# An audio tower of patch tokens, attention and routed experts on one core: places in five products, one joint inverse deviation, and another order of the first two rounds

## The reference, cut to what matters

```python
# tokenizer: x is (128, 1000, 16); 124 patches of 16 steps x 16 features at stride 8
y = einsum('bpi,di->bpd', patches, W) + b           # 256 -> 256
h = (y - mean(y)) * rsqrt(var(y) + 1e-5) * gamma + beta
# attention over the 124 tokens of each of 128 sequences, one head of 256
a = layernorm(h)
q, k, v = a @ Wq.T + bq, a @ Wk.T + bk, a @ Wv.T + bv
h = h + softmax(q @ k.T / scale) @ v
# experts: 6, the two best of each token, three layers 256x256
f = layernorm(h)
p = softmax(relu(f @ rw1 + rb1) @ rw2 + rb2); top_w, top_i = top_k(p, 2)
g = softmax(top_w)
e = relu(relu(f @ w1 + b1) @ w2 + b2) @ w3 + b3     # per expert
h = h + sum(g * e[top_i])
```

## Time and profile before

| | |
|---|---|
| median of three runs | 1258.8 us (1256.7 to 1262.85) |
| the profiled execution's own time | 1265.46 us |
| its span | 1263.7 us |
| instructions | 28188 |
| granted TensorE clock, mean | 0.981 |
| busy: PE, PEld, DVE, ACT, POOL | 96%, 85%, 79%, 71%, 73% |
| stage A (round 5 to 31) | about 101 to 557 us |
| end of stage A mixed with the first tiles | to about 665 us |
| stage B alone | 665 us to the end |

### The profile page before, as it was taken

One profiled execution on the slowest core, in us unless ns is written; L12 is line 12 of the kernel. 1 busy time (PEld: TensorE's weight loads), 2 busy tenths in 40 slices (PEclk: granted clock), 3 DMA queues, 4 the chain that ended last, 5 costly groups with the idle time before them and its releaser, 6 DMA issues.

```text
span 1263.7 us, 28188 instructions
## 1 busy us (share of the span) xinstructions
PE 1207.0 (96%) x7888; PEld 1073.8 (85%) x7888; DVE 998.4 (79%) x3283; ACT 894.7 (71%) x2094; POOL 918.5 (73%) x740
## 2 busy tenths in 40 slices
PE   4899999999999999999779999999999999999994
PEld 4799888988889888988668888888988888888883
DVE  4578888888889888887677878787777878777783
ACT  3688888888888888886446676666667666666762
POOL 2127888888888888888788676777677767766776
PEclk9899999999999999999898999999999999999997
DMA  3234555645445545654489979767786696787655
GB/s 101 85 123 123 151 154 158 153 124 127 124 127 130 131 122 134 180 160 120 130 184 267 243 137 219 133 108 128 148 199 116 114 234 116 128 192 156 115 60 58
DMA packets 137191, 180.44 MB, mean 143 GB/s; under 512 B 38344, under 2 KB 103500, under 8 KB 137036
## 3 DMA queue, kind: packets, MB, share of 16 engines
q0 software_dynamic: 75456, 69.19, 34.3%
q1 hardware_dynamic: 60316, 108.67, 28.5%
q10 hardware_dynamic: 1264, 0.79, 0.2%
HBM read 159.01 MB, written 101.49 MB: 206 GB/s over the span
## 4 chain that ended last, share of the span: by engine, by line
PE 86%; DVE 5%; ACT 4%; issue 3%; POOL 1%; DMA 0%; POOLq 0%; SPq 0%; ACTq 0%; DVEq 0%
PE bank L784 29%; PE bank L580 18%; PE bank L811 15%; PE bank L773 4%; PE bank L729 4%; PE bank L715 4%; PE bank L631 4%; PE bank L622 2%; PE bank L672 2%; PE bank L737 2%; PE bank L707 1%; PE bank L659 1%; ACT rec L885 1%; ACT square L920 1%; DVE h L1188 1%
## 5 line engine op out<-in xcount | busy, mean ns | idle before, releaser
L566 POOL DMA_INDIRECT out<-yo,tail x268 | 431.3, 1609 | 173.3 <-issue 139.9
L517 POOL DMA_INDIRECT expert_rows<-rec,row_i x256 | 358.5, 1401 | 72.8 <-issue 61.0
L995 ACT ACTIVATE h2v<-bank,small 128x512 f32<-128x512 f32 x134 | 92.3, 690 | 205.2 <-PE bank L784 190.6
L811 PE MATMUL bank<-w_sb,h_hi 128*128 128x256 f32 x1072 | 210.2, 289 | 3.0 <-issue 3.0
L784 PE MATMUL bank<-h_hi,w_sb 128*128 128x512 f32 x536 | 178.8, 394 | 7.6 <-issue 7.6
L784 PE MATMUL bank<-x_hi,w_sb 128*128 128x512 f32 x536 | 178.3, 394 | 4.6 <-DVE x_lo L1366 4.6
L811 PEld LDWEIGHTS bank<-w_sb,h_hi 128*128 128x128 f32 x1072 | 172.6, 193 | 3.7 <-issue 3.6
L811 PE MATMUL bank<-w_sb,h_lo 128*128 128x256 f32 x536 | 152.2, 284 | 0.0
L784 PEld LDWEIGHTS bank<-h_hi,w_sb 128*128 128x128 f32 x536 | 102.0, 190 | 28.1 <-issue 8.0
L784 PEld LDWEIGHTS bank<-x_hi,w_sb 128*128 128x128 f32 x536 | 101.8, 190 | 26.2 <-issue 4.9
L1381 DVE CAST h_hi<-h1v 128x512 fp32r<-128x512 f32 x134 | 63.2, 472 | 71.1 <-ACT h1v L988 71.1
(11 more groups left out here) (198 smaller groups left out, 3034.1 us busy)
## 6 DMA issues: line engine op xcount, KB each, us to landing
w_sb<-split_weights SPq DMA_DIRECT2D x189, 512.0 KB
xg<-expert_rows SPq DMA_DIRECT2D x67, 530.0 KB
out<-h SPq DMA_DIRECT2D x32, 496.0 KB
split_weights<-half_w SPq DMA_DIRECT2D x36, 256.0 KB
small<-in_esmall SPq DMA_DIRECT2D x67, 134.0 KB
x_in<-in_x SPq DMA_DIRECT2D x32, 250.0 KB
expert_rows<-pad_rows SPq DMA_DIRECT2D x9, 530.0 KB
raw_w<-in_eweights SPq DMA_DIRECT2D x36, 128.0 KB
```

Source lines behind the costliest of these rows:

```text
L517: pool.indirect_dma_start(rows_dram, bass.IndirectOffsetOnAxis(ap=row_i[0:TOK, slot, j, k:k + 1], axis=0), rec[0:TOK, slot, j, :], None).t ...
L566: pool.indirect_dma_start(out, bass.IndirectOffsetOnAxis(ap=tail[:, t % TAILS, j, E8:].bitcast(I32), axis=0), yo[:, t % YO, j, :], None, c ...
L811: mm = pe.matmul(banks[6 + b][:, (j % 2) * D:(j % 2 + 1) * D], act[:, c, j * P:(j + 1) * P], w[:, 2, c, wh, :], start=(c == 0 and p == 0), ...
L995: act.activation(h2v[:, m, :], banks[bank + m][:], ACT.Relu, bias=small[:, t % SLOTS, DC + m:DC + m + 1]).then_inc(S["h2_v"], 1)
```

## The change

- The places are made by five products. `picked` gets a fifth block of eight columns, always zero; the triangular product and four products with ones run over 40 columns, so that the fifth block of the result is the total of the group.
- GpSimd makes the inverse deviations of norm 0 (group of xa) and norm 2 (group of x2) in one pair of operations over both, behind norm 1's inverse and all three leftover scatters. ScalarE's squares are scaled by D ** -0.5 and put their sum into `mv`, where the other norms keep their variance. The three semaphores become `rstd13` and `rstd2`.
- VectorE compares the expert numbers as they come from `max_index`, without the copy `choice`, and makes the token numbers in one operation.
- At the start the token weight is centred by one sum and one fused operation, without waiting for the bias. The bias is loaded into a cleared tile (SP waits for GpSimd's first memset) and is handled behind the weight and behind the first input halves on both engines.
- `fold` is cut in two on TensorE and VectorE. On TensorE the first part stands ahead of round 0's token products and the second behind them. On VectorE the first part and `nmr` (now `shifts`) stand behind the statistics of x0, ahead of the input and chunk halves; the second stays at the end of the round.

```diff
+        def deviations(it):
+            return 2 * (it + 2)
...
             sp.dma_start(proj_raw["tok"][:], ...).then_inc(S["tok_loaded"], 16)
+            sp.wait_ge(S["pool_const"], 1)
             for r in (0, 32):
-                sp.dma_start(bias_raw["tok"][r:r + 1, :], tok_b).then_inc(S["tok_loaded"], 16)
+                sp.dma_start(bias_raw["tok"][r:r + 1, :], tok_b).then_inc(S["tok_bias_loaded"], 16)
...
+            pool.memset(bias_raw["tok"][0:33, :], 0.0).then_inc(done, 1)
...
+            def inverse_std(norms, ready, n):
+                count = len(range(NORMS)[norms])
+                pool.tensor_scalar(vareps[0:TOK, norms, :], mv[0:TOK, norms, :, 1], EPS, None, ALU.add).then_inc(ready, 1)
+                pool.wait_ge(ready, n * 2 + 1)
+                pool.tensor_tensor(rstd[0:TOK, norms, :], vareps[0:TOK, norms, :],
+                                   neghalf[0:TOK, :].unsqueeze(1).to_broadcast([TOK, count, GB]), ALU.pow
+                                   ).then_inc(ready, 1)
...
-                    inverse_std(1, S["rstd2"], g)
+                    inverse_std(slice(1, 2), S["rstd2"], g)
                 if x5:
-                    scatter(x5[0], range(5, 7))
+                    scatter(x5[0], range(5, 8))
                 if xa:
                     wait_apart(pool, S["squares"], (g + 1) * GB, S["pool_passed"])
-                    inverse_std(0, S["rstd1"], g)
-                if x5:
-                    scatter(x5[0], range(7, 8))
                 if x2:
                     wait(pool, S["xn2_ready"], g * GB)
                     wait_apart(pool, S["av"], g * AV_N + 1 + 3 * GB, S["pool_passed"])
-                    inverse_std(2, S["rstd3"], g)
+                if xa or x2:
+                    inverse_std(slice(0, NORMS, 2) if xa and x2 else slice(0, 1) if xa else slice(2, NORMS),
+                                S["rstd13"], it + 1)
...
+                if it == 0:
+                    fold_weights()          # TensorE, ahead of the token products
                 if xa:
                     if it == -1:
-                        pe.wait_ge(S["proj_low"], 2)
+                        pe.wait_ge(S["proj_low"], 1)
...
+                            if it == -1:
+                                pe.wait_ge(S["proj_low"], 2)
                             mm = pe.matmul(into, ones_r[:, 0:TOK], bias_row["tok"][:], start=False, stop=True)
                 if it == 0:
-                    fold()
+                    fold_rest()
...
-                    W = GB * E8
+                    W = (GB + 1) * E8
                     pe.matmul(banks[3][0:TOK, 0:W], before[0:TOK, 0:TOK], picked[0:TOK, :], start=True, stop=False, ...)
-                    for k in range(1, GB):
-                        pe.matmul(banks[3][0:TOK, k * E8:W], ones[0:TOK, 0:TOK], picked[0:TOK, 0:W - k * E8], ...)
-                    for k in range(GB):
-                        mm = pe.matmul(banks[3][0:TOK, W:W + E8], ones[0:TOK, 0:TOK], picked[0:TOK, k * E8:(k + 1) * E8], ...)
+                    for k in range(1, GB + 1):
+                        mm = pe.matmul(banks[3][0:TOK, k * E8:W], ones[0:TOK, 0:TOK], picked[0:TOK, 0:W - k * E8], ...)
...
+                if it == -2:                # ScalarE, behind xT_hi of group 0
+                    act.wait_ge(S["centred"], 2)
+                    high_halves("tok")
+                    act.wait_ge(S["centred"], 4)
+                    act.wait_ge(S["pool_const"], 3)
+                    high_bias("tok")
...
                         act.activation(square[0:TOK, :], ..., ACT.Square,
-                                       accum_out=sumsq[0:TOK, j:j + 1]).then_inc(S["squares"], 1)
+                                       scale=D ** -0.5, accum_out=mv[0:TOK, 0, j, 1:2]).then_inc(S["squares"], 1)
...
                 v.tensor_reduce(tok_mean[:], proj_raw["tok"][:], AX_X, ALU.add).then_inc(s, 1)
-                v.tensor_scalar(tok_mean[:], tok_mean[:], 1.0 / D, None, ALU.mult).then_inc(s, 1)
-                for c in range(DC):
-                    v.tensor_scalar(proj_raw["tok"][:, c, :], proj_raw["tok"][:, c, :], tok_mean[:, c:c + 1], None,
-                                    ALU.subtract).then_inc(s, 1)
+                v.scalar_tensor_tensor(out=proj_raw["tok"][:], in0=tok_mean[:].unsqueeze(2).to_broadcast([P, DC, D]),
+                                       scalar=-1.0 / D, in1=proj_raw["tok"][:], op0=ALU.mult, op1=ALU.add).then_inc(s, 1)
...
                     statistics(1, ...)      # VectorE, x0
+                if it == 0:
+                    fold_weights()
+                    shifts(0)
...
+                if it == -2:                # VectorE, behind xT_lo of group 0
+                    low_halves("tok", 1)
+                    centre_bias()
+                    low_bias("tok", 2)
+                    v.wait_ge(S["pool_const"], 22)
...
-                v.tensor_copy(choice[R, :, :], mxi[R, :, 0:TOPK]).then_inc(s, 1)
-                                choice[R, :, :].unsqueeze(3).to_broadcast([TOK, GB, TOPK, E8]),
+                                mxi[R, :, 0:TOPK].unsqueeze(3).to_broadcast([TOK, GB, TOPK, E8]),
...
-                v.tensor_copy(rec[R, g % SENT, :, D + E8:REC].bitcast(I32), tokid[R, :].unsqueeze(2)).then_inc(s, 1)
-                v.tensor_scalar(tokid[R, :], tokid[R, :], float(GT), None, ALU.add).then_inc(s, 1)
+                v.tensor_scalar(rec[R, g % SENT, :, D + E8:REC].bitcast(I32), tokid[R, :].unsqueeze(2), float(g * GT), None,
+                                ALU.add).then_inc(s, 1)
```

More of the change, by code:

```diff
@@ L60 @@
 SMALL = 2 * DC + D + E8
-LN1_N, AV_N, TOPK_N, POS_N = 15, 14, 25, 4
+LN1_N, AV_N, TOPK_N, POS_N = 15, 14, 23, 4
 ADDED = 16 * TB
@@ L69 @@
 PADS_AT, TABLE_AT = 1, 20
+NORMS = 3
 DRAIN = G + 1
@@ L472, in _ @@
             pool.memset(ones[:], 1.0).then_inc(done, 1)
-            pool.wait_ge(done, 6)
+            pool.wait_ge(done, 7)
             pool.affine_select(out=ident[:], in_=ident[:], compare_op=ALU.not_equal, fill=1.0, base=0,
@@ L493, in _ @@
             pool.memset(xg[:, 0, :, :], 0.0).then_inc(done, 1)
-            pool.wait_ge(done, 18)
+            pool.wait_ge(done, 19)
             pool.iota(xg[:, 0, :, D + E8:REC].bitcast(I32).rearrange("p j o -> p (j o)"), [[1, TB]], base=NTOK + TILE,
@@ L498, in _ @@
                       channel_multiplier=TB).then_inc(done, 1)
-            def inverse_std(which, ready, g):
-                if which == 0:
-                    pool.tensor_scalar(vareps[0:TOK, which, :], sumsq[0:TOK, :], 1.0 / D, EPS, ALU.mult,
-                                       ALU.add).then_inc(ready, 1)
-                else:
-                    pool.tensor_scalar(vareps[0:TOK, which, :], mv[0:TOK, which, :, 1], EPS, None,
-                                       ALU.add).then_inc(ready, 1)
-                pool.wait_ge(ready, g * 2 + 1)
-                pool.tensor_tensor(rstd[0:TOK, which, :], vareps[0:TOK, which, :], neghalf[0:TOK, :],
-                                   ALU.pow).then_inc(ready, 1)
+            pool.memset(picked[:], 0.0).then_inc(done, 1)
+            def inverse_std(norms, ready, n):
[5 more added lines that the diff above has]
+                                   ).then_inc(ready, 1)
             def scatter(g, pieces):
@@ L581, in product, with fold_weights @@
                 return mm
-            def fold():
-                one = ones_r[:].bitcast(F32)
+            one = ones_r[:].bitcast(F32)
+            def fold_weights():
                 pe.wait_ge(S["const_loaded"], N_CONST)
@@ L1063, in statistics, with fold_weights @@
                     v.bn_aggr(mv[R, which, j, :], stats[R, which, j, :]).then_inc(s, 1)
-            def fold():
+            def fold_weights():
                 s = S["fold_sb"]
+                v.reciprocal(invs_col[:], scale_col[:]).then_inc(S["invs"], 1)
                 v.wait_ge(S["fold_ps"], 1)
@@ L1174, in step @@
                                     half_w[:, n % RING, 0, :].bitcast(F32), ALU.subtract).then_inc(S["w_low"], 1)
-                if x0:
-                    g, slot, rnd = x0
-                    v.wait_ge(S["rstd2"], g * 2 + 2)
-                    v.scalar_tensor_tensor(out=nmr[R, 0, :], in0=mv[R, 1, :, 0], scalar=-1.0, in1=rstd[R, 1, :],
-                                           op0=ALU.mult, op1=ALU.mult).then_inc(S["ln1"], 1)
+                if x0 and it > 0:
+                    shifts(x0[0])
                 if it == DRAIN - 2:
@@ L1206, in step @@
                 if it == 0:
-                    v.wait_ge(S["const_loaded"], N_CONST)
-                    v.reciprocal(invs_col[:], scale_col[:]).then_inc(S["invs"], 1)
-                    fold()
-                    low_halves("v", 4)
-                    v.wait_ge(S["proj_high"], 5)
+                    fold_rest()
+                    low_halves("v", 3)
+                    v.wait_ge(S["proj_high"], 4)
                     v.tensor_tensor(proj["q"][:, 1, :, :], qk_raw[:], proj["q"][:, 0, :, :].bitcast(F32),
```

(4 more changed lines are left out.)

77 lines of the change are left out of this document (31 added, 46 removed).

## The result

The changed kernel takes **1249.6 us** (median of five runs, 1248.2 to 1249.8), the kernel before beside it on the same chip 1260.6 us (five runs, 1256.7 to 1262.9). The ratio is 0.9913, with a 95% interval of 0.9895 to 0.9931: 11.0 us less, where 11.7 were forecast. The profiled execution took 1249.82 us around a span of 1248.0; against the profiled one of before (1265.46) that is 15.6 us. Where the other 4.6 us come from has to be found before the difference of the two traces is read as the effect of the change.

The account below looks back on a forecast made before the run. Bounds: TensorE's order at the start, then a two-round loop of TensorE and ScalarE. Start 8.4, products 3.1 and VectorE 0.2 sum to 11.7 us: 1258.8 - 11.7 = 1247.1 us, range 1241.5 to 1254.5.

Parts of the forecast that it names:

- Centring: Start: a shorter VectorE path to the first token product gains 2.85 us, an earlier weight 0.3; first product at 9.15.
- Order of rounds 0 and 1: Start: half of `fold` fills TensorE's 2.6 us hole; with centring 8.4 us gained, first transposes of normalised tokens ending at 30.2.
- The rival that the start gives half: Start: the clock stays at 1.2 GHz through the folded products, gain 4.6 us, 1250.9 us in all; chance 0.17.
- The rival that the chunk loads gate round 1: Rounds 0 to 3: weight chunk loads hold round 1, 3.3 us of the start's gain remain, 1255.5 us; chance 0.13.
- Products: Rounds: five products save TensorE 0.17 us each, half counting in 24 rounds, all in seven: 3.1 us.
- the loop: Full rounds: TensorE and ScalarE hold each other over two rounds, 17.66 us a round before, 17.575 after.
- The rival that TensorE alone counts: Rounds: the three saved products come back in full, 5.4 us, 1244.8 us in all; chance 0.08.
- VectorE: Rounds: dropping `choice` (0.57 us) and one token-number operation gains nothing in full rounds, 0.2 us in the drain.
- Joint inverse: GpSimd's rounds: one eight-element pow of 1.9 us replaces two pairs; cost 0 if the pow takes under 2.6 us.
- The slower rival: GpSimd's rounds: a joint pow of 3.3 us makes GpSimd set the round, 1264 us in all; chance 0.07.
- One sign of failure: Rounds: the prediction is wrong if `nmr` of norm 2 waits for GpSimd; no size given.
- End of stage A: Where tiles and the last groups mix: waits for loads move with the rest; wrong if its length changes by over 2 us.

Follow-up runs that it names:

- start only: The kernel before with only the new centring and the new order of rounds 0 and 1: 1252.0 us, ratio 0.9934.
- five only: The kernel before with five products in place of eight and nothing else: 1257.5 us, ratio 0.9978.
- eight products: The changed kernel with the eight products of before: 1253.3 us, ratio 0.9937.
- one ScalarE copy: The changed kernel with one more ScalarE copy, read by nobody, behind the router's ReLU in each round: 1253.4 us, ratio 0.9946.
- split inverse: The changed kernel with norm 0's and norm 2's inverses apart and the old order of scatters: 1249.5 us, ratio 0.9928.
- nmr first: The changed kernel with VectorE's `shifts` put ahead of its chunk half: 1248.7 us, ratio 0.9917.

## Why the prediction was right

*Centring.* 2.85 and 0.3 us were taken; 2.9 measured, as the difference of two experiments. The first product starts at 8.97 for 9.15, the sum at 6.02 for 6.1. The first bias product, taken as free, comes some 0.2 us late (10.54).

*Order of rounds 0 and 1.* 5.3 us were taken (8.4 less 3.1), 5.0 to 5.3 measured. The sum 8.4 stands beside 8.1 for *start only*. The profile shows more: the transposes end at 28.99, not at 30.2, and group 1 is ahead by 9.6. The prediction took the low clock for all of group 0's products, 6.1 us, and they took 5.0 (8.97 to 13.97), because the clock rose within them. The 1.5 us between 9.6 and the medians' 8.1 are most likely the clock too, which rose late in the profiled execution of before; *five only* shows the same start 2.8 us ahead. The rival that the start gives half falls with the row at 12.31: from there the pairs are short, and they stay so through the folded products and group 1. The rule of the Trainium skill ("TensorE: Matmul & The Clock Gate", Part 1) that activity releases the clock agrees with this trace. The same part says that the number of slow matmuls of one kernel varies from run to run, which the prediction did not take in, and of which before and *five only* are a case.

*The gain travels.* Groups 1 to 5 take 69.10 us for 69.18, and with the start alone the gain at group 25 (9.8) is that of group 1 (9.6). The rival that the chunk loads gate round 1 falls.

*Products.* Half of 0.17 in rounds with a chunk, all of it in the others: 0.085 (*five only*) and 0.078 (*eight products*) measured where 0.085 follows from the loop, and 0.17 between groups 29 and 30. The term 3.1 us stands beside 2.6 of *five only* and, of *eight products*, 3.0 by the ratios and 3.7 by the medians. The rival that TensorE alone counts would have given 5.4 and falls. What holds the loop was named rightly, by *one ScalarE copy*: 0.20 us more on ScalarE is 0.09 us a round. The changed kernel's rounds are 17.528 for the 17.57 forecast, and the kernel before's 17.619 for the computed 17.66: the sum of the loop is 0.04 too long in both, which falls out of the difference. The 17.71 has gone, but rounds still alternate, 17.45 and 17.61, in some stretches of the trace.

*VectorE.* Nothing in ordinary rounds, and the wait went from 1.14 to 1.62. The prediction took 0.2 us for the drain; no run tells that from nothing. What it missed is the round with the table of tiles, 0.7 us shorter in the trace; the median can't show so little.

*Joint inverse.* Cost nothing that can be measured: 1.67 us for 1.9, and *split inverse* has the same time. The slower rival falls. One sign of failure did come, in small: `nmr` of norm 2 waits for GpSimd three times from 40 to 560 us, 1.6 us in all, each time before 150 us. As a sign it was badly chosen, for the kernel before has four such waits, the one near 67 us and three behind 520, 1.2 us in all. What the prediction missed is the effect of a shorter GpSimd program on where its instructions are loaded: 1.5 to 2.3 us between groups 5 and 6, and no difference of the times.

*End of stage A.* The prediction called itself wrong if this stretch changed by more than 2 us; it changed by 4.4. That step failed as written, but most likely not through the change: the 8.6 us wait and the low clock behind it are in the one profile of before. *Start only* has neither and takes 127.52, *five only* a wait of 1.4 us and a shorter stretch at the low clock, and takes 129.05, and each has a part of the change only. A second profile of before, which would settle it, wasn't taken. This would also account for the profiles: the one of before was 4.9 us above its median, by a late clock at the start and by this wait, so only about 11 of the 15.6 us are the change. The prediction had set the difference against the median and not against the profile. Of the 2.5 us by which its 1247.1 misses, 1.8 are the median of before, 1260.6 beside the changed kernel for the 1258.8 shown, and 0.7 the difference itself.

All terms: 8.1 by *start only* and 2.6 by *five only* are 10.7, and the ratios' 8.3 and 2.8 are 11.1, beside 11.0 for the whole. Nothing that can be measured is left for the joint inverse and the small edits. It is in part luck that the sum is so close. The term of the start was taken from a profile whose clock rose late, which makes it too large by some 1.5 us, and it took group 0's products 1.1 us too long, which makes it too small; the two nearly cancel. And the intervals of the two experiments are 1.4 and 1.6 us to either side. No version here beats the changed kernel by what can be measured.

## What to carry to other kernels

Here work put into a hole of TensorE at the start was paid twice: the 4.5 us of folded products went where a hole of 2.6 us had been, and the products of group 1 behind them took 3.6 us (18.43 to 21.99) where before they took 5.1, because the clock stayed up. The gain travelled through a pipeline whose rounds are full. Where two engines hold each other over two rounds, time taken from either counted by half, and in full in a stretch without the other. Look at single rounds before a mean of them is compared: one odd round in fifteen hid what *nmr first* did. And compare a second profile, or the medians, before a difference of traces is explained: here nearly a third of it was, most likely, one late load and one late rise of the clock.

## What was not expected of the hardware

- The granted clock rose at different moments in two executions of the same start: 16 matmuls or 32 from 20 to 24 us, 2.8 us at group 1. It also fell behind holes of 2.4 us (changed kernel: pairs of 0.63 us again from 29.43) and 2.6 us (before: from 22.20).
- GpSimd stood still for 4.0 to 4.4 us in the eight traces with this program length, around a transfer of its instructions, at a point that 24 further instructions ahead of it moved away.
- GpSimd's pow takes 1.05 us for 4 elements a partition and 1.67 for 8: as an estimate from these two, 0.15 us an element and some 0.4 of start.
